# A ring of three PSUM banks for transposes and side products, and the value product of a pair in one piece

## The reference

```python
# layer 1, one pass of four heads and one of the joined output
h = einsum('bnc,hdc->bhnd', x, Wh)
scores = einsum('...nd,...md->...nm', h, h)          # dot-product attention
attn = softmax(where(mask, scores, NEG))
out = einsum('...nm,...md->...nd', attn, h) + b
# layers 2 and 3
e = s_i[:, :, None] + s_j[:, None, :]                # additive attention
e = where(e >= 0, e, slope * e)
out = einsum('bij,bjd->bid', softmax(where(adj > 0, e, NEG)), h)
```

## Time and profile before

| | |
|---|---|
| median of 3 runs | 5710.56 us (5706.2 to 5715.72) |
| the profiled execution | 5713.95 us |
| its span | 5712.2 us |
| TensorE matmul / weight load busy | 5265.8 / 4508.6 us (92% / 79%) |
| DVE, ACT, POOL busy | 4372.0, 3731.8, 1942.3 us |
| mean granted TensorE clock | 0.978 |

### The profile page before, as it was taken

One profiled execution on the slowest core, in us unless ns is written; L12 is line 12 of the kernel. 1 busy time (PEld: TensorE's weight loads), 2 busy tenths in 40 slices (PEclk: granted clock), 3 DMA queues, 4 the chain that ended last, 5 costly groups with the idle time before them and its releaser, 6 DMA issues.

```text
span 5712.2 us, 132229 instructions
## 1 busy us (share of the span) xinstructions
PE 5265.8 (92%) x52922; PEld 4508.6 (79%) x52922; DVE 4372.0 (77%) x7325; ACT 3731.8 (65%) x5501; POOL 1942.3 (34%) x1724
## 2 busy tenths in 40 slices
PE   8499999999999899999999999999999999999966
PEld 6388787888878788887878878787888878788755
DVE  5677678778787877778787787878788787877866
ACT  3266557676676757667576666767576675767665
POOL 3400025133341523325241343415233252413466
PEclk9799999999999999999999999999999999999988
DMA  5200000000000000000000000000000000000000
GB/s 177 61 16 11 18 9 9 9 14 14 9 9 11 17 12 7 9 18 12 15 5 10 17 14 9 9 11 16 11 9 9 18 12 15 5 9 18 13 1 5
DMA packets 138241, 95.95 MB, mean 17 GB/s; under 512 B 96032, under 2 KB 115104, under 8 KB 137632
## 3 DMA queue, kind: packets, MB, share of 16 engines
q1 hardware_dynamic: 137632, 87.49, 6.1%
HBM read 35.55 MB, written 8.91 MB: 8 GB/s over the span
## 4 chain that ended last, share of the span: by engine, by line
PE 67%; issue 12%; DVE 6%; POOLq 6%; DVEq 2%; ACT 2%; POOL 1%; DMA 0%; SPq 0%; ACTq 0%
PE po L1067 22%; PE tp L1042 22%; PE pss L1030 9%; PE pss L1031 9%; POOLq L257 6%; DVE pt L1333 3%; DVE rows L1321 2%; PE px L988 2%; DVEq L257 1%; PE px L1055 1%; PE px L1005 1%; ACT rows L1234 1%; PE px L969 1%; PE px L1015 0%; POOL shut L866 0%
## 5 line engine op out<-in xcount | busy, mean ns | idle before, releaser
L1042 PE MATMUL tp<-ident,rows 128*128 128x128 f32 x14336 | 1948.1, 278 | 234.5 <-DVE pt L1333 193.3
L1333 DVE COPY pt<-tp 128x512 f32<-128x512 f32 x2048 | 1332.8, 686 | 921.1 <-PE tp L1042 912.1
L1234 ACT ACTIVATE rows<-rows,nm 128x2048 f32<-128x2048 f32 x896 | 1795.0, 2003 | 323.3 <-DVE nm L1321 321.2
L1042 PEld LDWEIGHTS tp<-ident,rows 128*128 128x128 f32 x14336 | 1600.9, 141 | 476.8 <-issue 308.2
L1067 PE MATMUL po<-pt,hn 128*64 128x128 f32 x28672 | 1782.8, 278 | 37.5 <-ACT ot L1195 36.3
L1067 PEld LDWEIGHTS po<-pt,hn 128*64 128x64 f32 x28672 | 1568.5, 138 | 192.4 <-issue 191.7
L1186 ACT COPY pt<-tp 128x512 f32<-128x512 f32 x1536 | 837.9, 589 | 769.7 <-PE tp L1042 760.9
L869 POOL TENSOR_TENSOR rows<-sr,mask 128x2048 f32<-128x2048 f32 x256 | 1048.7, 4098 | 514.7 <-PE tp L1042 508.4
L1030 PE MATMUL pss<-ha 128*128 128x512 f32 x2560 | 1062.9, 415 | 13.1 <-DMA ha<-hb 12.0
L1031 PE MATMUL pss<-ha,hb 128*128 128x512 f32 x2560 | 1009.5, 394 | 0.0
L1321 DVE CUSTOM_DVE_ANT_0 rows<-pss,mask,nm 128x1024 f32<-128x1024 f32 x640 | 821.7, 1284 | 88.2 <-issue 3.5
(11 more groups left out here) (108 smaller groups left out, 3220.6 us busy)
## 6 DMA issues: line engine op xcount, KB each, us to landing
hb<-ha SPq DMA_DIRECT2D x164, 128.0 KB, 2.3
ha<-hb SPq DMA_DIRECT2D x164, 128.0 KB, 2.3
adjb<-in_adj SPq DMA_DIRECT2D x32, 512.0 KB, 5.6
xin<-x SPq DMA_DIRECT2D x36, 128.0 KB, 2.5
xb<-in_x SPq DMA_DIRECT2D x16, 256.0 KB, 3.0
x<-t SPq DMA_DIRECT2D x16, 256.0 KB, 2.4
xb<-x SPq DMA_DIRECT2D x8, 512.0 KB, 4.0
out<-xb SPq DMA_DIRECT2D x32, 128.0 KB, 1.9
```

Source lines behind the costliest of these rows:

```text
L1042: last = nc.tensor.transpose(tp[q % 2][:, r * P:(r + 1) * P], rows[:, row.slot, jb * P:(jb + 1) * P], ident[:])
L1234: nc.scalar.activation(rows[:, row.slot, :], rows[:, row.slot, :], ACT.Exp, scale=-1.0, bias=nm[:, row.place, 1:2], accum_out=rs[:, row.pl ...
L1333: nc.vector.tensor_copy(pt[:, CH * q:CH * (q + 1), row.k % SLOTS, :], tp[q % 2][:].rearrange("p (j n) -> p j n", n=P)).then_inc(pt_dve, 1)
```

## The change

- The banks `tp0`, `tp1` and `px` become one ring of three, `ring0` to `ring2`. Every use (a turned tile, a back turn, a side product) takes the next bank in turn, and waits for the copy of the use three before it (`take`, `give`, `handed`). `Segment` numbers the uses beforehand, so that ACT and DVE know which bank to read (`tile_of`).
- `sum_values` does both halves of the pair in step s + 4 of the odd row, one after the other.
- ACT copies the sums of heads straight to `zt` instead of `ot`, and POOL multiplies there in place. ACT's wait for POOL before that copy goes.
- What stood before the first step becomes a segment of its own, `START`.

```diff
+BANKS = 3
+SIDE = ("xn", "xt", "proj", "hn", "h", "r")
...
+        uses = []
+        for s in self.steps:
+            turned = self.row(s - 2)
+            uses += self.side_uses(s)
+            uses += [("turn", turned.k, q) for q in (0, 1) if turned]
+            uses += [("back", r.pair) for r in (self.back(s),) if r]
+            uses += self.side_uses(s + 0.5)
+            uses += [("turn", turned.k, q) for q in (2, 3) if turned]
+        self.use = {key: n for n, key in enumerate(uses)}
...
-        tp = [ctx.enter_context(nc.psum_tensor(f"tp{i}", [P, BANK], F32)) for i in range(2)]
+        ring = [ctx.enter_context(nc.psum_tensor(f"ring{i}", [P, BANK], F32)) for i in range(BANKS)]
         po = ctx.enter_context(nc.psum_tensor("po", [P, BANK], F32))
-        px = ctx.enter_context(nc.psum_tensor("px", [P, BANK], F32))
...
-                    nc.gpsimd.tensor_tensor(dst, ot[:], ob[:].rearrange("p r n -> p (r n)"), ALU.mult)
+                    nc.gpsimd.tensor_tensor(dst, dst, ob[:].rearrange("p r n -> p (r n)"), ALU.mult)
...
-            def px_free():
-                if px_copied[0] is not None:
-                    wait(px_copied[0])
+            def take(*key):
+
+                n = taken[0]
+                assert where[0][0].use[key] + where[0][1] == n, key
+                taken[0] += 1
+                if freed[n % BANKS]:
+                    pe.wait_ge(*freed[n % BANKS])
+                return ring[n % BANKS]
+
+            def give(count, n):
+
+                freed[(taken[0] - 1) % BANKS] = count.sem, n
...
             def turn(row, q):
 
-                if q >= 2:
-                    wait_copy(row, q - 2)
-                elif row.before:
-                    wait_copy(row.before, q + 2)
+                tile = take("turn", row.k, q)
                 for r in range(CH):
                     jb = CH * q + r
-                    last = nc.tensor.transpose(tp[q % 2][:, r * P:(r + 1) * P],
+                    last = nc.tensor.transpose(tile[:, r * P:(r + 1) * P],
                                                rows[:, row.slot, jb * P:(jb + 1) * P], ident[:])
                 last.then_inc(tr_ready, 1)
+                count = copied[row.copier[q]]
+                give(count, count.n + row.count[q] + 1)
...
-                px_free()
-                nc.tensor.transpose(px[:, 0:P], turned, ident[:]).then_inc(back_ready, 1)
-                px_used(back_c)
+                tile = take("back", row.pair)
+                nc.tensor.transpose(tile[:, 0:P], turned, ident[:]).then_inc(back_ready, 1)
+                handed(back_c)
...
-                    if segment.odd(s - 3):
-                        sum_values(segment.odd(s - 3), 0)
                     if segment.odd(s - 4):
+                        sum_values(segment.odd(s - 4), 0)
                         sum_values(segment.odd(s - 4), 1)
...
             def take_sums(row):
 
+                wait(pv_c, pv_c.n + row.pair + 1)
+                if row.unit < H:
+                    nc.scalar.copy(zt[:, row.unit, row.t // 2, :], po[:, 0:P]).then_inc(ot_ready, 1)
+                    return
                 if row.pair or back_c.n:
-                    used = out_c if where[0].behind_head(row) else back_c
-                    wait(used, used.n + row.pair)
-                wait(pv_c, pv_c.n + row.pair + 1)
+                    wait(back_c, back_c.n + row.pair)
                 nc.scalar.copy(ot[:], po[:, 0:P]).then_inc(ot_ready, 1)
```

More of the change, by code:

```diff
@@ L104, in __init__ @@
         blocks = [r for r in self.rows if r]
-        for before, row in zip([None] + blocks, blocks):
-            row.slot_user, row.before = row.k - RING, before
+        for row in blocks:
+            row.slot_user = row.k - RING
         own = [r for r in blocks if r.k < self.blocks]
@@ L115, in __init__, with side_uses @@
             self.tasks.setdefault(step, []).append((name, unit, c))
-        assert all(k == "before" or int(k) in self.steps for k in self.tasks), self.tasks.keys()
+        assert all(int(k) in self.steps for k in self.tasks), self.tasks.keys()
+        uses = []
[7 more added lines that the diff above has]
+        self.use = {key: n for n, key in enumerate(uses)}
+        assert len(self.use) == len(uses)
+    def side_uses(self, key):
+        return [task for task in self.tasks.get(key, []) if task[0] in SIDE]
     def tasks_at(self, step):
@@ L141, in sequence @@
     def sequence(self):
-        return [(s, *task) for s in sorted(k for k in self.tasks if k != "before") for task in self.tasks[s]]
+        return [(s, *task) for s in sorted(self.tasks) for task in self.tasks[s]]
     def tally(self, *names):
@@ L162, in prologue @@
     order = [pair for u, hn in ((0, 1), (1, 2), (2, 1), (3, 2)) for pair in pairs_of(u, hn)] + [None] * GAP
-    tasks = [("before", "xn", 0, c) for c in range(NC)]
-    tasks += [("before", name, 0, g) for g in range(2) for name in ("proj", "low", "hn")]
+    tasks = []
     for u in range(H - 1):
@@ L173, in prologue, with start @@
     return Segment(order, False, True, tasks)
+def start():
+    tasks = [(0, "xn", 0, c) for c in range(NC)]
+    return Segment([], False, False, tasks + [(0, name, 0, g) for g in range(2) for name in ("proj", "low", "hn")])
 def next_head(first):
@@ L233, in epilogue @@
     return Segment(order, True, False, tasks)
-PROLOGUE, LOOP, EPILOGUE = prologue(), main_loop(), epilogue()
+START, PROLOGUE, LOOP, EPILOGUE = start(), prologue(), main_loop(), epilogue()
 class Count:
@@ L247, in run_segments @@
 def run_segments(run):
+    run(START)
     run(PROLOGUE)
@@ L956, in run_task @@
                 if name == "xn":
-                    px_free()
+                    px = take(name, unit, c)
                     xin_c[c % 2].n += 16
@@ L1073, in run_segment @@
             def run_segment(segment):
-                for task in segment.tasks.get("before", ()):
-                    run_task(*task)
+                where[0] = segment, taken[0]
                 for s in segment.steps:
@@ L1134, in next_of, with tile_of @@
                 wait(count)
+            where, used = [None], [0]
+            def tile_of(*key):
+                return ring[(used[0] + where[0].use[key]) % BANKS]
             def run_task(name, unit, c):
@@ L1172, in run_task @@
                     nc.scalar.mul(sr[:, cols], px[:], SLOPES[unit]).then_inc(sr_ready, 1)
-            where = [None]
             def hn_of(unit):
-                return [r.hn for r in where[0].rows if r and r.unit == unit][0]
+                rows_of = where[0].rows if where[0].blocks else PROLOGUE.rows
+                return [r.hn for r in rows_of if r and r.unit == unit][0]
             def copy_tile(row, q):
@@ L1202, in take_back @@
                 nc.scalar.copy(ob[:].rearrange("p r n -> p (r n)"),
-                               px[:, 0:P]).then_inc(back_copied, 1)
+                               tile_of("back", row.pair)[:, 0:P]).then_inc(back_copied, 1)
             def lift_row(row, half):
@@ L1244, in run_segment @@
                         take_sums(segment.odd(s - 4))
+                used[0] += len(segment.use)
                 read_c.n += 2 * segment.blocks
@@ L1333, in copy_tile @@
                 nc.vector.tensor_copy(pt[:, CH * q:CH * (q + 1), row.k % SLOTS, :],
-                                      tp[q % 2][:].rearrange("p (j n) -> p j n", n=P)).then_inc(pt_dve, 1)
+                                      tile_of("turn", row.k, q)[:].rearrange("p (j n) -> p j n", n=P)).then_inc(pt_dve, 1)
             def bend_block(row):
```

35 lines of the change are left out of this document (16 added, 19 removed).

## The result

The changed kernel takes 6622.43 us (median of 4; 6618.31 to 6624.08) against 5712.09 before: a ratio of 1.159, 95% interval 1.157 to 1.161. It is 910 us slower. The sign and the mechanism were as forecast, the size was not: 6330 was 290 too low, and 6622 lies above the range (6150 to 6480). The profiled execution has a span of 6619.3.

The account below looks back on a forecast made before the run. TensorE, busy 92% of the span, was taken as the bound. 5714 plus 172 + 20 + 214 + 75 + 17 + 15 = 513 gave 6227; with 100 for the clock, forecast 6330 us, range 6150 to 6480.

Parts of the forecast that it names:

- The saving of the joined product: TensorE, dot-product pairs: one uninterrupted product and run of turns saves 0.25 us a pair, 112 us over 448 pairs.
- Dot-product pairs: Odd step's first tile waits for ACT's back copy behind the exponential: a plain pair takes 11.87 us, 0.5 more.
- the mixed stretch: Stretch of each batch mixing additive and dot-product pairs: 178.5 us today, 209 after; +30, times 7 = +214.
- 172 + 20: Dot-product pairs outside the mixed stretch: +172 us for 264 pairs, +20 for side products that wait in the first tile's place.
- my mean of 0.65: Mean extra us per dot-product pair over three cases: plain 0.5, after a wide reciprocal 1.1, with side product 0.3.
- Additive pairs without the clock: Additive steps: first tile waits for the back copy; a pair takes 13.6 or 12.8 us, a dot-product pair behind it 12.6.
- The clock: Idle of 3 to 5 us in additive pairs lowers TensorE's clock; one in four of 128 pays: 100 us.
- rival 1: The clock falls in every additive pair: 128 pairs at 2.9 us = 370, so 6600 us; chance 0.15.
- 6227: Sum in us of all terms over the whole kernel, without the clock: 5714 plus 513.
- Its sign: What would show rival 1 in the profile: a granted clock below 0.9 on the mean.
- The six ADD2 pairs: Six additive pairs at the end of ADD2: 72.0 us now, 83 after; +11, times 7 = +75.
- What goes: TensorE's 193.3 us of waits for DVE's copy of tile 2 in additive steps, counted as inside the stretches' differences.

Follow-up runs that it names:

- e4: Changed kernel with extra transposes that nobody reads, 36 or twice 16 per additive even step, where TensorE would wait for the back copy: 6377.14 us, ratio 1.117.
- e2: Kernel before with one edit, both halves of the value product in the later step, banks as before: 6287.41 us, ratio 1.101.
- e1: Changed kernel, but ACT copies the back turn right behind tiles 0 and 1, ahead of lifts and exponential: 6053.01 us, ratio 1.060.
- e3: Changed kernel with the value product split over two steps again, the ring of banks kept: 5999.31 us, ratio 1.051.
- e6: Changed kernel with the value product split over two steps and ACT's back copy ahead of lifts and exponential: 5694.33 us, ratio 0.997.
- e9: As e6, but TensorE does the back turn directly behind tiles 0 and 1, ahead of the half product: 5641.21 us, ratio 0.987.

## Why the prediction was wrong in size and right in kind

- **The saving of the joined product** (0.25 a pair) is there in the plain pair: the product takes 3.65 instead of 3.80, and tiles 0 and 1 of the even step take 0.87 instead of 0.97. It doesn't shorten the whole, since the waits that follow cost more.
- **Dot-product pairs.** 11.87 forecast, 11.89 measured. The 264 pairs outside the mixed stretch were costed at 172 + 20. The prologue (21 of it) took 26.5 more; steps 8 to 32 and 64 to 80, 140 pairs and 91 by my mean of 0.65, took 84 more. Right in the sum; the pair at step 22 lost 27 of the 84, and most others less than the mean.
- **Additive pairs without the clock.** From first tile to first tile, dot products of the next row included, 13.57 + 1.93 = 15.5 was forecast; in e4, where the clock stays up, the pair at step 36 measured 107.7 / 7 = 15.4. The dot-product pair behind it: 12.57 - 1.93 = 10.6 forecast, 74.1 / 7 = 10.6 measured. Right, to the copy of tile 1 behind the scores.
- **The clock: the step that failed.** I took "one in four of the 128 additive pairs" and 100 us. e4 puts some 245 on it, and each of the 112 additive pairs of the seven loops is 1.3 to 3.1 us longer than in e4, where the clock stays up: all of them pay. My argument against, that 241 waits leave the clock at 0.978 today, came from waits mostly under 1 us (179 of them) and said nothing on 4.7. That every additive pair pays was rival 1, at 0.15. Its 6600 is near the result partly by luck: it priced the clock at 370, too much, on a sum of 6227, too low. Its sign, a mean clock below 0.9, did not come either: the mean is 0.919, though the clock falls in every additive pair. Its rule, the Trainium skill's TensorE: Matmul & The Clock Gate, HAM oscillation (gaps between bursts set the array back each time), agrees with the trace: 0.75 behind the 4.72 us gap. The fallen clock covers part of the steps only, so it cost 1.35 us in the pair shown, not 2.9, and 1.9 on the mean of the 128 (245 / 128).
- **What was not in the sum:** without the clock I had 6227, and e4 took 6377: a second error of 150 us. In e4 steps 80 to 100 take 167 more than before, where I had some 53 (17 and 56 pairs at 0.65). There the pairs at steps 88 and 98 alone lost 40 and 49 over the seven loops, by an overlap of DVE with POOL that the prediction doesn't have. It is read in the last section, and no run tested it alone. The mixed stretch took 267 more instead of 214: 214.1 a loop where I had 209, and 176.0 before on the mean where the loop that I read had 178.5. The six ADD2 pairs took 92 more instead of 75.
- **"What goes"**: I charged the joined product for waits for copies in dot-product steps only. e2 shows that it costs 577 by itself, with 442 of waits for DVE in place of 193. In the changed kernel that loss hides behind the wait for `ob`; e1 uncovers it. So the two edits' losses (577 and 289) don't add up to 910 exactly: 866, and each pulls the clock down (0.945 and 0.948). No run took the sums' new way to `zt` or the start segment by itself; e3 has both.

## What to carry to other kernels

Before several users share a ring of buffers, ask for each user who frees the bank and what stands ahead of that release on its engine; a bank that one engine frees behind a long operation makes every later user wait for that operation. A piece of work may be the cover for the copies of the tiles before it: the halves of the product in two steps covered such waits in both, and joining them saved 0.25 us a pair and cost more. Where TensorE is to idle for several us at a time, price what stands behind every gap at the lower clock: here each additive pair of the loops paid 1.3 to 3.1 us. And when a step gets shorter, look for the long operations that it lets start earlier, and for what they then run beside.

## What the runs showed of the hardware that was not expected

Filler work can pay: 4212 transposes that nobody reads took 245 us off, since they kept the clock at 0.975.

A DVE operation with two inputs in SBUF can stand for as long as a POOL operation runs. In the steps 88 and 98 of a loop of the changed kernel:

```profile
3657.66 4.62 POOL L886 TENSOR_TENSOR rows<-sr,mask 128x2048 f32<-128x2048 f32 x1 [9.95 <-PE ring L1064]
...
3658.35 4.48 DVE L1317 TENSOR_TENSOR ha<-hc,hb 64x512 fp32r<-64x512 f32 x1
...
3662.86 1.29 DVE L1366 COPY pt<-ring 128x512 f32<-128x512 f32 x2
...
3663.70 1.94 PE L1064 MATMUL ring<-ident,rows 128*128 128x128 f32 x8 [2.97 <-DVE pt L1366]
...
3731.66 4.08 POOL L886 TENSOR_TENSOR rows<-sr,mask 128x2048 f32<-128x2048 f32 x1 [8.99 <-PE ring L1064]
...
3731.83 4.19 DVE L1337 TENSOR_TENSOR xb<-xb,y 128x256 f32<-128x256 f32 x1
...
3737.68 1.11 PE L1064 MATMUL ring<-ident,rows 128*128 128x128 f32 x4 [2.88 <-DVE pt L1366]
```

The median of the subtraction in step 88 is 0.69 us; here it took 4.48 and ended 0.55 after POOL's mask row (3662.28). The addition in step 98 has a median of 0.43 and took 4.19. Both happen in all seven loops of the changed kernel and of e1, e2 and e4, and in no loop of the kernel before, e3, e6 and e9, where the product is split. Before, in step 88, the step was longer, POOL got its free row later (3198.38) and DVE was done first (3197.48 + 0.69). So a shorter step on TensorE released POOL into DVE's way, and DVE's late copy made TensorE wait 2.97, and 2.88 in step 98. The Trainium skill, SBUF — State Buffer, Who interferes with whom, says that a DVE instruction with two SBUF inputs contends with a GpSimd instruction that reads SBUF; these rows agree.
